# One kernel of two transformer layers: constants filled by DMA in an earlier stage, two first-in-line moves, and a wider GpSimd multiply

## The reference

```
def L0_attn_a(x):                                  # 16 heads of width 8 for each of 4 sequences
    v = x @ v_w + v_b
    kern = ...                                     # a curve over distance for each head, from sin() of positions
    causal_kern = ALPHA * step(kern) * window
    scores = causal_kern[i - j] + qm[i] + km[j] + MIX * (qc @ kc.T) / sqrt(8)
    ctx = softmax(where(i >= j, scores, -1e9)) @ v
    h = layernorm(x + ctx @ out_w + out_b)
    return layernorm(h + gelu(h @ ffn_w1 + ffn_b1) @ ffn_w2 + ffn_b2)

def L1_attn_b(x):                                  # 16 heads of width 64, one shared key and value head
    sim = scale * q @ k.T + bucketed_bias[j - i] * 8
    return softmax(causal(sim)) @ v @ Wout + bout
```

## Time and profile before

| | us |
|---|---|
| three runs, median (lowest to highest) | 3712.45 (3709.52 to 3714.45) |
| the profiled execution | 3700.37 |
| its span in the trace | 3698.6 |
| project, table stage (from the trace) | 12.8 to 119, 119 to 237 |
| two-pass attention | 237 to 882 |
| L1 attention b, its rounds | 2582 to 3446 |

### The profile page before, as it was taken

The page is one execution under the profiler, slowest core; times in us unless marked ns, Lnnn a source line. Parts: engine busy times, 40 slices in busy tenths (PEclk is TensorE's granted clock), DMA queues, the critical chain, the costliest instruction groups (busy, mean ns, idle before and its releaser), DMA issues. The chain is left out here.

```text
span 3698.6 us, 67338 instructions
## 1 busy us (share of the span) xinstructions
PE 3090.0 (84%) x25109; PEld 1695.7 (46%) x25109; DVE 2374.2 (64%) x5080; ACT 1844.5 (50%) x3304; POOL 1010.2 (27%) x803
## 2 busy tenths in 40 slices
PE   5487777774859999797699978998989888999899
PEld 2123333331347555573222226764444544554676
DVE  5567777772856455564499953225988888888222
ACT  3115555553336323363289943433655565655344
POOL 1409888894100223000000000001222222222100
PEclk8679999997979899896599978999999999999999
DMA  4212232221032000132422210006524334322000
GB/s 136 86 60 75 75 109 77 98 79 33 13 120 115 1 1 1 47 130 83 143 64 65 68 47 10 1 9 220 107 73 102 90 95 99 90 80 71 27 10 12
DMA packets 214263, 260.64 MB, mean 70 GB/s; under 512 B 45213, under 2 KB 164473, under 8 KB 211622
## 3 DMA queue, kind: packets, MB, share of 16 engines
q1 hardware_dynamic: 213975, 256.78, 23.1%
HBM read 200.66 MB, written 56.55 MB: 70 GB/s over the span
## 5 line engine op out<-in xcount | busy, mean ns | idle before, releaser
L1174 POOL TENSOR_TENSOR l0aa_e<-l0aa_e,l0aa_et 128x512 f32<-128x512 f32 x432 | 535.7, 1275 | 97.8 <-ACT l0aa_e L1317 97.8
L2523 ACT ACTIVATE l1ba_sg<-l1ba_sg,l1ba_mn 128x128 f32<-128x128 f32 (+7 forms) x512 | 393.3, 769 | 243.4 <-DVE l1ba_mn L2575 242.3
L1345 DVE TENSOR_REDUCE l0aa_low<-l0aa_pP 128x8 f32<-128x1024 f32 x288 | 342.1, 1220 | 153.1 <-PE l0aa_pP L1198 152.3
L2575 DVE CUSTOM_DVE_ANT_0 l1ba_sg<-l1ba_pS,l1ba_tab 128x128 f32<-128x128 f32 (+7 forms) x512 | 368.8, 745 | 86.4 <-PE l1ba_pS L2463 64.2
L2584 DVE STREAM_TRANSPOSE l1ba_pT<-l1ba_sg 128x1024 f32<-128x1024 f32 (+3 forms) x344 | 367.1, 1067 | 37.1 <-PE l1ba_pO L2483 34.5
L319 PEld LDWEIGHTS f_pY<-l_w,f_hT 128*128 128x128 f32 x2048 | 268.1, 192 | 124.1 <-issue 118.8
L2483 PE MATMUL l1ba_pO<-l1ba_pT,l1ba_v 32*64 32x256 f32 x9216 | 314.8, 388 | 5.5 <-ACT l1ba_y L2538 4.6
L2411 POOL TENSOR_TENSOR l1ba_co<-l1ba_co,l1ba_rb 128x1024 f32<-128x1024 f32 x64 | 150.9, 2357 | 610.1 <-ACT l1ba_co L2531 545.4
L2940 ACT ACTIVATE l1aa_e<-l1aa_e 128x1536 f32<-128x1536 f32 x192 | 284.4, 1483 | 41.9 <-DVE l1aa_e L2981 25.3
L2463 PE MATMUL l1ba_pS<-l1b_k,l1ba_qs 64*128 64x384 f32 (+3 forms) x1024 | 262.2, 593 | 47.0 <-DVE l1ba_mn L2575 35.3
L1317 ACT ACTIVATE l0aa_e<-l0aa_pS 128x512 f32<-128x512 f32 x432 | 252.8, 592 | 82.1 <-PE l0aa_pS L1231 48.0
(11 more groups left out here) (405 smaller groups left out, 5202.3 us busy)
## 6 DMA issues: line engine op xcount, KB each, us to landing
f_wB<-l0f_weights SPq DMA_DIRECT2D x16, 2048.0 KB, 7.2
l1ba_rb<-l1b_rdd SPq DMA_DIRECT2D x64, 512.0 KB
l0aa_et<-l0a_table SPq DMA_DIRECT2D x16, 1536.0 KB, 7.6
l1b_qd<-l1bp_part SPq DMA_DIRECT2D x64, 256.0 KB, 2.3
l1ba_qs<-l1b_qd SPq DMA_DIRECT2D x64, 256.0 KB
l0aa_et<-l0a_table SPq DMA_DIRECT2D x16, 512.0 KB, 8.1
l1ba_tab<-l1b_table SPq DMA_DIRECT2D x32, 256.0 KB, 5.2
l1ba_qs<-l1b_qd SPq DMA_DIRECT2D x64, 128.0 KB
```

The source lines that it names most:

```text
L1174: nc.gpsimd.tensor_tensor(es, es, t, ALU.mult).then_inc(multiplied, 1)
L1345: nc.vector.tensor_reduce(low1[:, t, :], pP[TURN[quad, t]][:].rearrange("p (u t) -> p u t", t=P), AX.X, ALU.min).then_inc(p1_low, 1)
L2523: nc.scalar.activation(row, row, ACT.Exp, bias=mn[:, r % 2, i + k:i + k + 1], scale=-1.0, accum_out=den[:, r % 2, i + k:i + k + 1]).then_i ...
L2575: nc.vector.tensor_tensor_reduce(row, scores, bias, 1.0, 3e38, ALU.add, ALU.min, mn[:, r % 2, h:h + 1]).then_inc(m_done, 1)
```

## The change

Four edits.
1. The four memsets of the stacks, their waits and the three DMAs of ones leave the table stage. A new `fill_stacks` issues seven DMAs on SP in the project stage, behind `load_l0_ffn` and ahead of the first sends: the three of 3 partitions, and zeros into 42, 29, 42 and 29 partitions, each partition 12 x 2 KB. Its semaphore is waited for at the end of the project stage.
2. GpSimd multiplies heads 0 and 1 of a group in one instruction of 1024 columns (it waits for both exps), and head 2 in one of 512.
3. PE: F stands ahead of S(n+2) at even n instead of behind it.
4. ACT in L1 attention b: `out` stands ahead of `exps` of the same step.

```diff
-            for n in range(N):
-                g, j = n // QUAD, n % QUAD
-                if j != ADDED:
-                    pool.wait_ge(e_done, g * ADDED + j + 1)
-                    es, t = table_of(pool, n, e[:, n % E_SLOTS, :])
-                    nc.gpsimd.tensor_tensor(es, es, t, ALU.mult).then_inc(multiplied, 1)
+            for g in range(QUADS * NB):
+                quad, b = g // NB, g % NB
+                if b == 0:
+                    pool.wait_ge(et_in[quad % 2], 64 * (quad // 2 + 1))
+                for j, heads in ((0, 2), (2, 1)):
+                    pool.wait_ge(e_done, g * ADDED + j + heads)
+                    slot = (g * QUAD + j) % E_SLOTS
+                    es, t = e[:, slot:slot + heads, :], et[:, quad % 2, j:j + heads, TABLE_AT[b]:]
...
+                    nc.gpsimd.tensor_tensor(es, es, t, ALU.mult).then_inc(multiplied, heads)
...
             for n in range(N):
-                if n + RING - 1 < N:
-                    second_pass(n + RING - 1)
                 if n % 2 == 0:
                     quad, t = (n + AHEAD) // STEPS + 1, (n + AHEAD) % STEPS // 2
                     if quad < QUADS:
                         first_pass(quad, t)
+                if n + RING - 1 < N:
+                    second_pass(n + RING - 1)
...
+STACK_CONSTANTS = 7
+
+
+def fill_stacks(sp, D, qs, ks, ready):
+
+    for dst, name in ((qs[51:54], "minus_ones"), (ks[48:51], "ones"), (ks[MAX_ROWS:MAX_ROWS + 3], "ones"),
+                      (qs[54:MAX_ROWS], "zeros"), (qs[MAX_ROWS + 3:], "zeros"), (ks[54:MAX_ROWS], "zeros"), (ks[MAX_ROWS + 3:], "zeros")):
+        rows = dst.shape[0]
+        sp.dma_start(dst.rearrange("p s j t -> p (s j) t"), D[name][0:rows].unsqueeze(1).broadcast_to([rows, STACKS * 4, SEQ])).then_inc(ready, 16)
...
             load_l0_ffn(sp, D, C)
+            fill_stacks(sp, D, qs, ks, filled)
...
             sp.wait_ge(zeroed, 64)
+            sp.wait_ge(filled, 16 * STACK_CONSTANTS)
...
-            sp.wait_ge(zeroed, 4)
-            for dst, src in ((qs[51:54], "minus_ones"), (ks[48:51], "ones"), (ks[MAX_ROWS:MAX_ROWS + 3], "ones")):
-                sp.dma_start(dst.rearrange("p s j t -> p (s j) t"), D[src].unsqueeze(1).broadcast_to([3, STACKS * 4, SEQ])).then_inc(stacks_in, 16)
...
-            for i, stack in enumerate((qs, ks)):
-                nc.gpsimd.memset(stack[32:64], 0.0).then_inc(zeroed, 1)
-                pool.wait_ge(zeroed, 2 * i + 1)
-                nc.gpsimd.memset(stack[64:P], 0.0).then_inc(zeroed, 1)
-                pool.wait_ge(zeroed, 2 * i + 2)
...
-                if n < N:
-                    exps(n)
                 for r in range(ROUNDS):
                     if n == FIRST[r + 2] + 1:
                         out(r)
+                if n < N:
+                    exps(n)
```

More of the change, by code:

```diff
@@ L1168, in _ @@
             nc.gpsimd.memset(vh[:, :, :, U:, 16 + HD:16 + HD + 1], 1.0).then_inc(ones_set, 1)
-            for n in range(N):
-                g, j = n // QUAD, n % QUAD
-                if j != ADDED:
-                    pool.wait_ge(e_done, g * ADDED + j + 1)
-                    es, t = table_of(pool, n, e[:, n % E_SLOTS, :])
-                    nc.gpsimd.tensor_tensor(es, es, t, ALU.mult).then_inc(multiplied, 1)
+            for g in range(QUADS * NB):
[6 more added lines that the diff above has]
+                    es, t = e[:, slot:slot + heads, :], et[:, quad % 2, j:j + heads, TABLE_AT[b]:]
+                    if b == 7:
+                        es = es.rearrange("p h (a t) -> p h a t", a=2)
+                        t = t[:, :, 0:256].unsqueeze(2).broadcast_to([P, heads, 2, 256])
+                    else:
+                        t = t[:, :, 0:GROUP]
+                    nc.gpsimd.tensor_tensor(es, es, t, ALU.mult).then_inc(multiplied, heads)
         @block.tensor
@@ L1414, in l0_attn_a @@
             qs, ks = (inner.enter_context(nc.sbuf_tensor(f"{tag}_{n}", [P, STACKS, 4, SEQ], BF16)) for n in ("qs", "ks"))
-            l0a_project(nc, D, x, C, f"{tag}p", h0, v_all, pooled, qd, kd, qm, km)
+            l0a_project(nc, D, x, C, f"{tag}p", h0, v_all, pooled, qd, kd, qm, km, qs, ks)
             l0a_table(nc, D, C, f"{tag}t", pooled, mods, table, qs, ks, qd, kd, qm, km)
@@ L1420, in l0_attn_a, with l0a_project @@
         l0a_output(nc, D, x, C, f"{tag}o", h0, cx, den, out)
-def l0a_project(nc, D, x, C, tag, h0, v_all, pooled, qd, kd, qm, km):
+STACK_CONSTANTS = 7
[4 more added lines that the diff above has]
+        sp.dma_start(dst.rearrange("p s j t -> p (s j) t"), D[name][0:rows].unsqueeze(1).broadcast_to([rows, STACKS * 4, SEQ])).then_inc(ready, 16)
+def l0a_project(nc, D, x, C, tag, h0, v_all, pooled, qd, kd, qm, km, qs, ks):
     SCALE = -0.15 / 8 ** 0.5
@@ L1449, in l0a_project @@
         src = {"q": pQ, "k": pK, "m": f["m"]}
-        w_in, zeroed = sem("weights_in"), sem("zeroed")
+        w_in, zeroed, filled = sem("weights_in"), sem("zeroed"), sem("filled")
         ln_step, ln_ve, ln_rough = sem("ln_step"), sem("ln_ve"), sem("ln_rough")
@@ L1657, in l0a_table @@
             ("u_done", "f_step", "f_ready", "s_ready", "n_done", "sg_ready", "t_ready", "stored"))
-        b_ready, zeroed, stacks_in = sem("b_ready"), sem("zeroed"), sem("stacks_in")
+        b_ready, stacks_in = sem("b_ready"), sem("stacks_in")
         NW = 8
@@ L1682, in _ @@
             sp.wait_ge(stored, 32)
-            sp.wait_ge(stacks_in, 16 * (3 + STACKS * STACK_LOADS))
+            sp.wait_ge(stacks_in, 16 * STACKS * STACK_LOADS)
         @block.gpsimd
@@ L1687, in _ @@
             nc.gpsimd.memset(L[:], 0.0).then_inc(zero, 1)
-            pool.wait_ge(zero, 1)
-            for i, stack in enumerate((qs, ks)):
-                nc.gpsimd.memset(stack[32:64], 0.0).then_inc(zeroed, 1)
-                pool.wait_ge(zeroed, 2 * i + 1)
-                nc.gpsimd.memset(stack[64:P], 0.0).then_inc(zeroed, 1)
-                pool.wait_ge(zeroed, 2 * i + 2)
             nc.gpsimd.memset(tb[:, SEQ:], 1e30)
```

## The result

The changed kernel takes 3614.38 us (median; 3611.18 to 3624.34), the one before 3710.98 (3705.17 to 3714.45): a ratio of 0.9745, 95% interval 0.973 to 0.976, 96.6 us less. The forecast was 3685, 27 us less, in a range of 3608 to 3722. The time lies in the range, but the gain is over three times the forecast one.

The account below looks back on a forecast made before the run. Two-pass attention was taken as bound by the 3.99 us loop A, S, F, L, A, GpSimd close behind. Project +41, table -20, attention -12, L1 attention b -36 sum to -27: 3685 from a median of 3712.45, range 3608 to 3722.

Parts of the forecast that it names:

- the wait of X: Two-pass attention: X blocks DVE some 4.3 us in every quad until GpSimd is dry; GpSimd then idles 3.7 us.
- the term: Two-pass attention: wide multiply and F ahead of S together, -12 us, a quad 37.2 against 37.70.
- a loop of 3.2: Two-pass attention: with F ahead of S, the DVE and PE loop falls to about 3.2 us instead of 3.99.
- the forecast picture: Two-pass attention: X waits 4.3 us, GpSimd idles 3.7, PE restarts at half clock, a quad takes 37.2 us.
- X is not starved (3617): Two-pass attention rival: X waits one multiply at most, the ring of E slots absorbs it; -80 there, chance 0.18.
- Project, +41: Project stage: 804 rows of fills queue on one DMA engine, the sends land late, ACT starts 41 us later.
- The rival with the fills spread over all engines: Project stage: fills spread over all engines cost 0 instead of +41, 3644; chance 0.10 with the different-engines case.
- Table, -20: Table stage: two tiny operations of 9.72 and 10.15 us fall to 0.23 without the memsets, about 20 us less.
- L1 attention b, -36: L1 attention b: copies run first, so about four fifths of `project`'s 44.7 us wait for them goes, -36 us.

Follow-up runs that it names:

- one more multiply: The changed kernel with one more 512-column multiply of a scratch tile on GpSimd in each group; 3808.82 us in one execution.
- the one-operand X: The changed kernel with X reducing one SBUF operand, subtraction left out: 3606.71 us; the same X on the kernel before with only F moved ahead of S: 3640.48.
- the spread fills: The kernel before with only the stack fills moved, zeros in DMAs of 32, 10, 16 and 13 partitions instead of 42 and 29; 3705.54 us, ratio 0.9991.

## Why the prediction was right or wrong

**Two-pass attention, the step that failed.** The step is the wait of X. I wrote that X "doesn't get through while GpSimd has its next input ready", that after the change "its input is ready in every quad", and made of it a block of 2.1 + 2.2 = 4.3 us and a quad of 37.2. The runs showed X at 0.73 us in thirteen quads and a quad of 32.0, so the term is -75 and not -12. GpSimd's input was ready, and X got through all the same: what X waits for goes with how far ahead it is ready, and that was 0.85 us at the regular X, not the 2.1 that I had reckoned.

The rows of the kernel before could have told me. I read there that GpSimd "had been empty" when a regular X started at 493.37. It had not:

```profile
492.42 3.78 POOL L1174 TENSOR_TENSOR l0aa_e<-l0aa_e,l0aa_et 128x512 f32<-128x512 f32 x3 [0.47 <-ACT l0aa_e L1317]
```

It ran three multiplies without a gap. The first of them ended at 493.69, the input of the second had been ready since 493.37, 0.32 us ahead, and X ended at 493.84, just behind that end. So what I had in hand was a lead of 0.32 us at which X gets in and the last X, blocked from a lead of 1.19 us on. Between them I drew no line and took the change for the second, which was itself a border case, as shown above.

The size of the lead was wrong as well. It does not grow by 0.35 us a group, as I had reckoned from a loop of 3.2: at the starts of the wide multiplies of one quad it is 0.47, 0.86, 0.61, 0.82, 1.10, 1.09 and, in X's group, 0.14 us (exp 508.49, start 508.63). One, two and three groups before X the second multiply has leads of 1.56, 1.76 and 1.32 us, at which by the table above X would have gone on waiting. That X stands where the lead is low is luck, and I had not reckoned it. That ACT, DVE and PE are held to GpSimd's pace by W, which waits for the multiplies on PE ahead of later S, is how I read it; no run took that wait away. For edit 3 alone the forecast picture and the term were right, and with one more multiply X was blocked in every quad. With edits 2 and 3 the kernel is on the other side of the border.

The step to do was to ask how much GpSimd's speed itself changes the lead. With edit 3 alone a group costs it 3.69 us and the lead at X is 1.30 us and more, with edit 2 added 3.55 and 0.85; that the shorter time is the cause, and not where the ends of the wide multiplies fall, was not separated.

**Rival "X is not starved (3617)".** It named -80 and a quad of 32.45; measured are -74.6 and 32.0, and the time is 3614.38. That its 3617 is met to 3 us is in part luck: it has the prediction's other terms in it, and project 10 too small, table 11 too large, L1 attention b 9 too small and the 20 us between traces and medians happen to cancel. Its mechanism, one multiply at the most, holds for the thirteen regular X and not for the others. The Trainium skill ("SBUF — State Buffer", section "Who interferes with whom") has whoever issues first hold the shared port for the whole instruction, while the other is blocked; that is a wait for one instruction of the other. The 0.73 us of the regular X agrees, the 4.86 us over three ends (edit 3 alone) and the 9.59 us over six (one more multiply) do not, so here the measurement decides. What the same section states, that a DVE instruction with two inputs in SBUF contends with a GpSimd instruction that reads SBUF, and one with at most one such input, outside the modes that use two ports, does not, agrees with the one-operand X, 0.26 to 0.27 us in all sixteen quads, and with A.

**Project, +41 for +51.** The mechanism was right: 24.7 GB/s for one engine, and both 29-row fills on the same one, as the share stays at 0.07 and not at 0.13. Mis-sized was how fast that engine does its rows while the others have fills too. I let it run at 24.7 GB/s from 26 on. The ffn's loads were indeed over then (in the kernel before the DMA share from 26 to 30 is 0.01), but in the kernel after from 30 to 34 all DMA engines together moved 89 GB/s at a share of 0.89, so each went at a quarter of that rate:

```profile
30.00:34.00 4.00, 4.00 (x5) 0.86 (x4) 0.77 (x1) 0.00 (x0) 0.00 (x0) 1.00 0.89 89
```

The engine ended at 102 and not at 92.7; the trace does not show how much of these 9 us this stretch makes. The rival with the fills spread over all engines had this wrong too: it put their cost at 0, and the spread fills cost 12. And I had SP issue on without a halt; it could not, with its issues held up for 38 and 32 us, so group 0's last sends were issued at 97 to 101. The sends themselves then took 4 to 5 us against 4.1 forecast.

**Table, -20 for -9.** The rows named fell as forecast. What I missed is that the 20 us lay ahead of rounds which PE sets when its clock is at half. From the second sine round to the last, the serial chain between them included, the traces of the study show 67.8 us in one execution, 78.4 in seven, 87 in four and 94.5 in two (without edit 1 it is 87 or 94.5, with it 67.8 or 78.4); apart from that chain they differ in how many rounds take 7.31 us in place of 3.77. In the one of 67.8 (one more multiply) the whole 20 us was gained. So the clock gives this term its 7 to 11 us of play, and the prediction had none there.

**L1 attention b, -36 for -45.5.** Right mechanism, mis-sized: I kept a fifth of the 44.7 us as copies that wait for PE anyway, and all of it went. No new wait ate it up: DVE's waits for the score matmuls fell too (64.2 to 23.1 us on line 2575, now 2587).

**The sum.** Of the 70 us by which the median missed, the attention is 63, L1 attention b 9, table and project, which came out dearer, -11 and -10, and 20 lie between the profiled executions and the medians. That the time fell within the range at all is the first rival's doing, for whose 3617 the range had been drawn that wide.

## What to carry to other kernels

When an operation can be starved by a neighbour engine, its price is a step and not a slope. Ask how long before each end of the neighbour's operations its next input arrives, before and after the change. Here making only the suppliers faster (edit 3) brought the price on, and a cheaper multiply beside it (edit 2) took it away. And read the neighbour's own row at every place from which you take a rule: a single long case may stand on the border. Two edits that each measure nothing may be worth 2% together, so test them in pairs before one is thrown out. A DMA whose partition count has no large divisor up to 16 is better cut into ones that have (here 39 us), and put where nobody's sends stand behind it (here another 12).
